# Attention scores accumulated in one PSUM bank from differences of key tiles

## The chip, the cores and the metric

The kernel runs on one core of a Trainium2 chip. The metric is the device time of one execution in microseconds (us). The kernel before took 1691.6 us as the median of three runs (1691.25 to 1692.2).

Engines by the profile's names: PE is TensorE (matmuls; PEld is its loads of stationary weights), DVE is VectorE, ACT is ScalarE, POOL is GpSimd, SP is the engine that issues most DMAs. PSUM has eight banks of 512 float32 columns for each of 128 partitions.

## The reference

```python
xn = layernorm(x)                          # x: 2 x 2048 x 256
q, k, v = split(xn @ w_qkv)                # 16 heads of 16 dimensions
q, k = spectral_filter(q), spectral_filter(k)
attn = softmax(q @ k.T / 4)                # 2048 x 2048 for each of 32 (head, batch)
h = square(relu(xn @ W_fc.T)); y = h @ W_proj.T
spikes = mean of five leaky steps on y
out = x + (attn @ v) @ w_out + b_out + spikes
```

The spectral filter is folded into the query and key weights. All arithmetic is float32 in kind: queries and keys are split in a high and a low part, so that one pass of the faster matmul format on 64 rows (16 dimensions, four products of parts) gives a score.

## The kernel before, in words

A first stage of some 112 us normalises x, projects queries and keys (stored to a scratch in HBM, `qk_scratch`) and values, and finds maxima for the first head. The last stage, some 30 us, multiplies by `w_out` and stores. Between them lie 32 heads (16 heads, 2 batches each; "head" below means one of the 32), and the change is in these.

The softmax subtracts for each query the maximum over all keys. So each head's scores are computed twice. The first time queries lie on the partitions (`maximum`, L711, products of 64x512), and DVE reduces each row (L1017, L1023, L1036) to `pmax`. After half a head's maxima a chain of four short DVE operations (`split_shift`, L1058 to L1073) makes the negated maxima in two parts, and SP spreads them by 8 small DMAs (`store_shift`, L329) to `shift_rows`. These maxima run ahead of the scores by `LEAD`. The second time keys lie on the partitions: `scores` (L718) opens a sum in PSUM and `shifted` (L724) adds to it the product of ones with `shift_rows`. ACT takes the exponential (L562) to `probs`, and `times_v` (L735) multiplies by the values, of which a further column of ones gives the denominator.

One step is 128 keys by 1024 queries. A head has 32 steps. PE's order is written out by hand in `pair` (two steps): 4 products for maxima, 4 for scores, 4 for shifts, 4 product parts of the feed-forward layer (`up` L841, `down` L846), and 8 products with the values, each of 256 columns. All but the last kind use 64 of the 128 rows, and two of them, one in each half of the rows, run side by side. Products with the values use 32 of the columns each, and four run side by side; a float32 product shows as two records.

Six PSUM banks form three slots of two banks (`ring`), which rotate between maxima and scores. ACT copies half of every second slot of maxima to SBUF (`take_half`, L568) for DVE. Two more banks hold the attention output (`po`) and the feed-forward results (`misc`).

SP's queue is in order. In each head (function `head` of the SP block) it issues 8 DMAs of keys (L310), 8 of queries (L320), 16 of shifts (L329) and 8 that move the attention output (L339), with waits on `exp_done`, `shift_turned` and `out_turned` between them. POOL runs the five leaky steps and squares the feed-forward values.

Of the kernel before, what the change touches and what calls it, by code (L numbers as in the profile page):

```python
# [33 lines left out]
STEPS = 2 * TB  # L34
LEAD = 8
FIRST_MAX = 2 * (UNITS - LEAD)
ALONE = STEPS * (B * H - 1) + LEAD
LAG = 2
PRESETS = 7
WARM = 10  # L40
FIRST = 6
PS = 4
# [7 lines left out]
SHIFT = 8 * 16  # L50
SIDE = 4 * DH
SPIKES = 5
AFTER_COPY = (2, 10, 26)
# [16 lines left out]
def build(nc, x, wqk, wv, wout, bout, logits, wfc, wproj, dft, eye, out):  # L70
    with ExitStack() as ctx:
# [3 lines left out]
        def sem(name):  # L75
# [3 lines left out]
        qk_dram = nc.dram_tensor("qk_scratch", [2, H, DH, 2, TOK], F32, kind="Internal").ap()  # L79

# [6 lines left out]
        kst = [sb(f"kst{i}", [P, S], F32R) for i in range(2)]  # L87
        shift_rows = sb("shift_rows", [P, S], F32R)
        ones = sb("ones", [P, P], F32R)
        probs = sb("probs", [P, PS, HALF])  # L90
# [3 lines left out]
        wout_sb = sb("wout_sb", [P, KC, D])  # L94
        bout_sb = sb("bout_sb", [P, D])
# [9 lines left out]
        half_sb = sb("half_sb", [P, BLK])  # L105
# [13 lines left out]
        xt = probs[:, 0:2, :].rearrange("p b (k d) -> p b k d", k=KT)  # L119
        hilo = [[t.rearrange("p (c t) -> p c t", c=2) for t in  # L120
                 (probs[:, 2, :], probs[:, 3, :], relu_sb[:, :, :].rearrange("p f t -> p (f t)"),
# [11 lines left out]
        assert at <= NT * D // 2  # L133

# [15 lines left out]
        def late_copy(g):  # L150

            return FIRST < g < ALONE and g % STEPS in AFTER_COPY

        places = {}
        for g in range(0, STEPS * B * H, 2):
            if g >= ALONE:
                at = [places[ALONE - 2][1], places[ALONE - 2][2], places[ALONE - 2][0]]
                places[g] = (None, at[(g - ALONE) % 3], at[(g + 1 - ALONE) % 3])
            elif g == 0:
                places[g] = (0, 1, 2)  # L160
            else:
                even_max_at, even_score_at, odd_score_at = places[g - 2]
                places[g] = ((even_score_at, even_max_at, odd_score_at) if late_copy(g) else
                             (even_score_at, odd_score_at, even_max_at))

        def copies_until(g):
            return sum(late_copy(k) for k in range(0, g + 1, 2))

        def score_slot(g):
            return ring[:, places[g - g % 2][1 + g % 2], :]  # L170

        def unit_slot(g):
            return ring[:, places[g - g % 2][0], :]
# [114 lines left out]
        def _(sp):  # L288
# [57 lines left out]
            for t in range(NB):  # L346
# [8 lines left out]
                if t == NB - 2:  # L355
                    sp.wait_ge(preset, PRESETS)
                    store_shift(0, 0)
# [901 lines left out]
```

## Time and profile before

| | before |
|---|---|
| median of three runs | 1691.6 us |
| span of the profiled execution | 1689.3 us |
| PE busy (matmuls) | 1681.4 us, x17842 |
| PEld busy (weight loads) | 1145.9 us |
| DVE busy | 1494.2 us, x2375 |
| ACT busy | 1330.1 us, x1718 |
| POOL busy | 719.7 us |
| granted TensorE clock | 1.000 |
| DMA | 108.02 MB, mean 64 GB/s |

The span runs from the first to the last instruction of the profiled execution; its own time is not listed beside it, and the median of the runs is 2.3 us above the span. Busy time is the time in which at least one instruction of the engine was under way. Two matmuls that run side by side count once. In a row of the timeline the first number is the start, the second the length of the whole group (xN instructions), and the brackets give the idle time before it and what ended that.

### The profile page before, as it was taken

How to read it: one execution, taken by the hardware profiler on the slowest of the kernel's cores; microseconds unless marked ns; L12 is line 12 of the kernel's file. 1: busy time of each engine (PE TensorE's matmuls, PEld its weight loads, DVE VectorE, ACT ScalarE, POOL GpSimd, SP SyncE). 2: the span in 40 equal slices, each digit the busy share in tenths (PEclk: the TensorE clock that was granted, in tenths of full speed). 3: DMA queues.
4: the chain of work that ended last, by engine and by line, in shares of the span. 5: the costliest groups of instructions: out<-in, count | busy, mean ns of one | idle time of the engine just before them, and what ended most of it. 6: DMA issues, size and time to landing. Idle time of an engine off the chain costs nothing.

```text
span 1689.3 us, 44435 instructions
## 1 busy us (share of the span) xinstructions
PE 1681.4 (100%) x17842; PEld 1145.9 (68%) x17842; DVE 1494.2 (88%) x2375; ACT 1330.1 (79%) x1718; POOL 719.7 (43%) x979
## 2 busy tenths in 40 slices
PE   9999999999999999999999999999999999999999
PEld 6566666666666666666666666666666666666667
DVE  6889999998999999989998999999989998999884
ACT  5548888888888888888888888888888888888872
POOL 3103334555433345554333455543335554333455
PEclk9999999999999999999999999999999999999999
DMA  6851122112211221122112211221122112211133
GB/s 216 294 161 47 33 54 55 51 33 55 55 50 34 55 55 43 41 55 55 43 41 55 56 37 47 55 55 36 48 55 56 31 53 55 55 30 54 43 105 103
DMA packets 95406, 108.02 MB, mean 64 GB/s; under 512 B 56032, under 2 KB 70240, under 8 KB 95200
## 3 DMA queue, kind: packets, MB, share of 16 engines
q1 hardware_dynamic: 91744, 101.97, 21.2%
q10 hardware_dynamic: 3456, 3.21, 0.6%
q8 instruction: 141, 2.31, 0.6%
q14 instruction: 65, 0.53, 0.1%
HBM read 78.91 MB, written 20.97 MB: 59 GB/s over the span
## 4 chain that ended last, share of the span: by engine, by line
PE 98%; DVE 1%; ACT 0%; issue 0%; ACTq 0%; POOL 0%; POOLq 0%
PE banks L735 31%; PE ring L711 22%; PE ring L718 14%; PE ring L724 14%; PE banks L841 7%; PE banks L846 3%; PE banks L659 2%; PE ring L928 2%; PE ring L672 1%; PE ring L645 1%; PE ring L659 1%; PE ring L686 0%; DVE stats L947 0%; DVE attnT L979 0%; ACT xnT L513 0%
## 5 line engine op out<-in xcount | busy, mean ns | idle before, releaser
L562 ACT ACTIVATE probs<-ring 128x1024 f32<-128x1024 f32 x1024 | 1002.1, 1026 | 6.5 <-PE ring L724 6.2
L711 PE MATMUL ring<-kst,qst 64*128 64x512 f32 x2000 | 674.7, 417 | 0.3 <-ACT probs L562 0.3
L735 PE MATMUL banks<-probs,vst 128*32 128x256 f32 x8192 | 548.2, 385 | 0.1
L1036 DVE TENSOR_REDUCE pmax<-ring 128x2 f32<-128x1024 f32 x407 | 497.7, 1223 | 12.7 <-PE ring L711 0.5
L568 ACT ACTIVATE half_sb<-ring 128x512 f32<-128x512 f32 x500 | 299.2, 598 | 261.4 <-PE ring L711 254.1
L718 PE MATMUL ring<-qst,kst 64*128 64x512 f32 x2048 | 493.0, 425 | 0.1
L711 PEld LDWEIGHTS ring<-kst,qst 64*128 64x128 f32 x2000 | 328.3, 184 | 208.3 <-issue 204.6
L1017 DVE TENSOR_REDUCE pmax<-ring 128x1 f32<-128x512 f32 x500 | 345.4, 691 | 88.7 <-PE ring L711 85.1
L724 PE MATMUL ring<-shift_rows,ones 64*128 64x512 f32 x2048 | 422.9, 390 | 0.0
L1023 DVE TENSOR_REDUCE pmax<-half_sb 128x1 f32<-128x512 f32 x500 | 335.5, 671 | 37.0 <-ACT half_sb L568 33.1
L735 PEld LDWEIGHTS banks<-probs,vst 128*32 128x32 f32 x8192 | 213.7, 109 | 209.7 <-issue 91.0
L841 PE MATMUL banks<-xnT,wfc_sb 64*128 64x128 f32 x2024 | 331.7, 284 | 0.1
L464 POOL TENSOR_TENSOR lif<-lif 128x256 f32<-128x256 f32 x32 | 19.7, 614 | 729.6 <-ACT y_sb L586 729.6
L846 PE MATMUL banks<-wproj_sb,hid_sb 64*128 64x256 f32 x1024 | 329.0, 401 | 0.0
L841 PEld LDWEIGHTS banks<-xnT,wfc_sb 64*128 64x128 f32 x2024 | 280.6, 186 | 19.6 <-PE ring L711 0.4
L718 PEld LDWEIGHTS ring<-qst,kst 64*128 64x128 f32 x2048 | 233.4, 185 | 26.5 <-ACT probs L562 3.6
L724 PEld LDWEIGHTS ring<-shift_rows,ones 64*128 64x128 f32 x2048 | 214.8, 185 | 17.2
L846 PEld LDWEIGHTS banks<-wproj_sb,hid_sb 64*128 64x128 f32 x1024 | 169.6, 184 | 10.9
L474 POOL TENSOR_SCALAR lif<-lif 128x256 f32<-128x256 f32 x128 | 110.1, 860 | 10.8
L475 POOL TENSOR_SCALAR lif<-lif 128x256 f32<-128x256 f32 x128 | 110.6, 864 | 8.0
L473 POOL TENSOR_TENSOR lif<-lif 128x256 f32<-128x256 f32 x128 | 95.1, 743 | 10.0
L471 POOL TENSOR_TENSOR lif<-lif 128x256 f32<-128x256 f32 x128 | 94.3, 737 | 10.0
(96 smaller groups left out, 1050.9 us busy)
## 6 DMA issues: line engine op xcount, KB each, us to landing
kst<-qk_scratch SPq DMA_DIRECT2D x256, 128.0 KB, 3.0
qst<-qk_scratch SPq DMA_DIRECT2D x256, 128.0 KB, 2.9
qk_scratch<-attnT SPq DMA_DIRECT2D x32, 256.0 KB, 3.0
shift_rows<-shiftT SPq DMA_DIRECT2D x512, 2.0 KB
qk_scratch<-probs SPq DMA_DIRECT2D x16, 256.0 KB, 3.0
attnT<-o_turned SPq DMA_DIRECT2D x256, 16.0 KB, 1.9
xnT<-x SPq DMA_DIRECT2D x8, 512.0 KB, 5.6
out<-xnT SPq DMA_DIRECT2D x7, 512.0 KB, 2.9
```

Of the source, the lines that this page charges most:

```text
L475: pool.tensor_scalar(decayed, mem, BETA, None, ALU.mult).then_inc(lif_step, 1)
L562: act.activation(probs[:, s % PS, :], score_slot(g), ACT.Exp, scale=SCALE).then_inc(exp_done, 1)
L568: act.activation(half_sb[:], unit_slot(2 * p)[:, BLK:2 * BLK], ACT.Copy).then_inc(half_taken, 1)
L711: return pe.matmul(unit_slot(g)[:, c * BLK:(c + 1) * BLK], qst[b][rows, tile * P:(tile + 1) * P], kst[b][rows, key:key + BLK], start=True, ...
L718: pe.matmul(score_slot(g)[:, c * BLK:(c + 1) * BLK], kst[b][rows_of(side), kt * P:(kt + 1) * P], qst[b][rows_of(side), q:q + BLK], start=T ...
L724: mm = pe.matmul(score_slot(g)[:, c * BLK:(c + 1) * BLK], ones[rows_of(side), :], shift_rows[rows_of(side), q:q + BLK], start=False, stop= ...
L735: mm = pe.matmul(po[32 * j:32 * (j + 1), half * D:(half + 1) * D], vst[b][:, kt, :], quarters[:, j], start=(kt == 0), stop=(kt == TB - 1))
L841: return pe.matmul(misc[:, (f % 4) * P:(f % 4 + 1) * P], wfc_sb[rows_of(side), c, f * P:(f + 1) * P], xnT[rows_of(side), c, tile * P:(tile ...
L846: return pe.matmul(misc[:, 0:D], hid_sb[rows_of(side), f, :], wproj_sb[rows_of(side), f, :], start=(f == 0 and side == 1), stop=(f == FC - ...
L1017: dve.tensor_reduce(pmax[:, tile, 2 * part:2 * part + 1], unit_slot(g)[:, 0:BLK], AX, ALU.max).then_inc(mx_taken, 1)
L1023: dve.tensor_reduce(pmax[:, tile, 2 * part + 1:2 * part + 2], half_sb[:], AX, ALU.max).then_inc(half_max, 1)
L1036: dve.tensor_reduce(pmax[:, tile, 2 * part:2 * part + 2], unit_slot(g).rearrange("p (c e) -> p c e", c=2), AX, ALU.max).then_inc(mx_taken, 1)
```

## The change

Scores are now computed in places of 512 queries by 128 keys ("mini-steps", 64 in a head), each in one PSUM bank. Three banks (1, 4, 5) serve the scores in turn, three others (0, 2, 3) the maxima. In each quarter of 512 queries the first three key tiles are computed as before, a score product and a shift product (`first_score`). From the fourth on, the bank still holds the score of the key tile three before, shift included, and one product of the queries with the difference of the two key tiles is added to it (`next_score`). The exponential reads the bank between the two.

The differences come from a new path: SP loads the keys in 16 DMAs (`load_stage`), POOL subtracts and adds (`subtract_keys`), ACT rounds to the high part (`high_delta`), POOL makes the low part (`low_delta`), SP stores both in 8 DMAs (`store_delta`) and loads them in three pieces of 4 DMAs each to `delta_sb` (`load_delta`). That is for each head.

PE's order is written anew in groups of four mini-steps ("quads"): `opening_quad` once in each quarter, `later_quad` three times. Products with the values are made for four mini-steps together, of 128 columns each. DVE reduces each maximum's bank by itself (`next_max`), and the copies by ACT are gone. Beside the reductions DVE splits the shifts after mini-steps 15 and 47, takes the outputs from PSUM after 35 and after 3 of the next head, and turns them after 55 and after 23. `w_out` and `b_out` share their buffer with the staged keys and are loaded late.

```diff
-LEAD = 8
+LEAD = 16
-PS = 4
+PS = 8
+CHAINS = 3
+PLACES = 3
+SCORE_BANKS = (1, 4, 5)
+MAX_BANKS = (0, 2, 3)
...
+            def load_stage(u):
...
+                for seg in range(SEGS):
+                    for k in range(2):
+                        at = b * S + k * HOP + seg * SEG
+                        sp.dma_start(stage[seg * DH:(seg + 1) * DH, k, :, :],
+                                     qk_dram[1, h, :, :, at:at + SEG]).then_inc(staged, 16)
+            def store_delta(u):
...
+                for seg in range(SEGS):
+                    sp.dma_start(delta_dram[u % 2, :, :, seg * SEG:(seg + 1) * SEG],
+                                 delta_pair[seg * DH:(seg + 1) * DH]).then_inc(delta_stored, 16)
+            def load_delta(u, piece):
...
+                for group in range(4):
+                    sp.dma_start(delta_sb[group * 2 * DH:(group + 1) * 2 * DH, cols].bitcast(F32),
+                                 src).then_inc(delta_in[piece], 16)
...
             def head(h, b, last=False):
                 i = 2 * h + b
+                sp.wait_ge(exp_done, MINI * i + QUAD)
                 if i and not last:
...
                     load_keys(h + b, 1 - b, 1)
+                if not last:
+                    load_stage(i + 1)
                 store_shift(2 * i + 1, 1)
                 if i:
                     move_output(i - 1, 1)
                 if i and not last:
                     load_queries(h + b, 1 - b, 1)
                 if h < H - 1:
-                    sp.wait_ge(exp_done, STEPS * i + TB + 2)
+                    sp.wait_ge(exp_done, MINI * i + MINI // 2 + QUAD)
                     load_queries(h + 1, b, 0)
...
                 if not last:
+                    store_delta(i + 1)
                     store_shift(2 * i + 2, 0)
+                if h < H - 1:
+                    sp.wait_ge(exp_done, MINI * i + MINI - TB + QUAD)
+                    load_keys(h + 1, b, 0)
                 move_output(i, 0)
-                if h < H - 1:
-                    sp.wait_ge(exp_done, STEPS * i + TB + TB // 2 + 2)
-                    load_keys(h + 1, b, 0)
...
+                if not last:
+                    for piece in range(len(PIECES)):
+                        sp.wait_ge(exp_done, MINI * i + MINI - TB + (piece + 2) * QUAD)
+                        load_delta(i + 1, piece)
...
+            def maximum(x, side):
...
+                pe.wait_ge(mx_taken, n + 3 - PLACES)
+                pe.matmul(max_bank(x), qst[b][rows, tile * P:(tile + 1) * P], kst[b][rows, chunk * BLK:(chunk + 1) * BLK],
+                          start=True, stop=True).then_inc(mx_ready, 1)
+            def bank_free(g):
...
+                if g >= CHAINS:
+                    pe.wait_ge(exp_done, g + 1 - CHAINS)
+            def first_score(g, side):
...
+                bank_free(g)
+                pe.matmul(score_bank(g), kst[b][rows, kt * P:(kt + 1) * P], qst[b][rows, q:q + BLK],
+                          start=True, stop=False)
+                pe.matmul(score_bank(g), ones[rows, :], shift_rows[rows, q:q + BLK],
+                          start=False, stop=True).then_inc(score_ready, 1)
+            def next_score(g, side):
...
+                for piece, (lo, hi) in enumerate(PIECES):
+                    if m * P == lo + HOP:
+                        pe.wait_ge(delta_in[piece], PIECE * (u + 1))
+                bank_free(g)
+                at = (kt - CHAINS) * P
+                pe.matmul(score_bank(g), delta_sb[rows, at:at + P], qst[b][rows, q:q + BLK],
+                          start=False, stop=True, skip_group_check=True).then_inc(score_ready, 1)
+            def times_v(first, last):
+                pe.wait_ge(exp_done, last + 1)
...
+                    for j in range(4):
+                        mm = pe.matmul(po[32 * j:32 * (j + 1), quarter * P:(quarter + 1) * P], vst[u % 2][:, kt, :],
+                                       quarters[:, j], start=(kt == 0), stop=(kt == TB - 1))
...
+            def opening_quad(u, quarter):
+                g, near, far = MINI * u + TB * quarter, 1, 0
+                maximum(g, far)
+                first_score(g, near)
+                first_score(g + 1, far)
+                share(u, quarter, 0, 0)
+                share(u, quarter, 0, 1)
+                maximum(g + 1, far)
+                share(u, quarter, 0, 2)
+                maximum(g + 2, far)
+                share(u, quarter, 0, 3)
+                maximum(g + 3, far)
+                first_score(g + 2, near)
+                next_score(g + 3, far)
+                if g:
+                    times_v(g - QUAD, g - 1)
+            def later_quad(u, quarter, n):
+                g, near = MINI * u + TB * quarter + QUAD * n, 1 - n // 2
+                far = 1 - near
+                maximum(g, far)
+                next_score(g, near)
+                share(u, quarter, n, 0)
+                next_score(g + 1, far)
+                maximum(g + 1, far)
+                share(u, quarter, n, 1)
+                share(u, quarter, n, 2)
+                maximum(g + 2, far)
+                next_score(g + 2, far)
+                share(u, quarter, n, 3)
+                next_score(g + 3, near)
+                maximum(g + 3, far)
+                times_v(g - QUAD, g - 1)
```

## Rows read from the trace of the kernel before

**Rows 1.** Busy us by stretch: PE, PEld, DVE, ACT, POOL, clock, DMA share, GB/s.

```profile
800.00:900.00 100.00, 100.00 (x1130) 68.49 (x1132) 90.39 (x139) 82.72 (x106) 46.36 (x63) 1.00 0.18 47
```

**Rows 2.** Timeline (start, us, engine, line): one pair of steps, PE and DVE.

```profile
800.96 0.18 PEld L711 LDWEIGHTS ring<-kst,qst 64*128 64x128 f32 x1 [0.41 <-issue]
800.96 0.49 PE L711 MATMUL ring<-kst,qst 64*128 64x512 f32 x1
...
801.49 0.69 DVE L1017 TENSOR_REDUCE pmax<-ring 128x1 f32<-128x512 f32 x1 [0.20 <-PE ring L711]
...
803.00 0.59 PEld L735 LDWEIGHTS banks<-probs,vst 128*32 128x32 f32 x16
803.00 1.07 PE L735 MATMUL banks<-probs,vst 128*32 128x256 f32 x16
...
804.00 0.18 PEld L711 LDWEIGHTS ring<-kst,qst 64*128 64x128 f32 x1 [0.41 <-issue]
```

**Rows 3.** Timeline, last head: pairs without maxima, then without feed-forward parts too.

```profile
1642.35 1.07 PE L735 MATMUL banks<-probs,vst 128*32 128x256 f32 x16
...
1644.91 1.07 PE L735 MATMUL banks<-probs,vst 128*32 128x256 f32 x16
...
1652.15 1.07 PE L735 MATMUL banks<-probs,vst 128*32 128x256 f32 x16
...
1654.28 1.07 PE L735 MATMUL banks<-probs,vst 128*32 128x256 f32 x16
```

**Rows 4.** Timeline of PE from 803.0 to 803.3.

```profile
802.68 0.39 PE L711 MATMUL ring<-kst,qst 64*128 64x512 f32 x1
...
803.00 0.64 PE L735 MATMUL banks<-probs,vst 128*32 128x256 f32 x8
```

**Rows 5.** Timeline: a maximum, the split of the shifts, their first DMA.

```profile
807.56 0.69 DVE L1017 TENSOR_REDUCE pmax<-ring 128x1 f32<-128x512 f32 x1 [0.29 <-PE ring L711]
...
808.17 0.18 DVE L1058 TENSOR_REDUCE nmax<-pmax 128x8 f32<-128x32 f32 x1
...
808.92 0.65 DVE L1023 TENSOR_REDUCE pmax<-half_sb 128x1 f32<-128x512 f32 x1
809.03 0.67 SPq L329 DMA_DIRECT2D shift_rows<-shiftT  x1
```

**Rows 6.** Timeline: a weight load that waits for a reduction's bank.

```profile
107.00 1.28 DVE L1012 TENSOR_REDUCE pmax<-ring 128x1 f32<-128x512 f32 x2
107.73 0.19 PEld L645 LDWEIGHTS ring<-kst,qst 128*128 128x128 f32 x1 [0.62 <-DVE pmax L1012]
```

**Rows 7.** Timeline of ACT: 512 columns, then the next.

```profile
1617.78 0.60 ACT L573 ACTIVATE relu_sb<-banks 128x512 f32<-128x512 f32 x1
1618.25 1.04 ACT L562 ACTIVATE probs<-ring 128x1024 f32<-128x1024 f32 x1
```

**Rows 8.** Timeline of SP: shifts and outputs of one half head.

```profile
784.84 5.29 SPq L329 DMA_DIRECT2D shift_rows<-shiftT  x8
790.18 2.58 SPq L339 DMA_DIRECT2D attnT<-o_turned  x4
```

**Rows 9.** Timeline of SP: four DMAs of keys, four of queries.

```profile
165.57 1.82 SPq L310 DMA_DIRECT2D kst<-qk_scratch  x4
...
1592.27 2.51 SPq L320 DMA_DIRECT2D qst<-qk_scratch  x4
```

**Rows 10.** DMA issues: KB each, median us from issue to landing.

```profile
kst<-qk_scratch SPq DMA_DIRECT2D x256, 128.0 KB, 3.0
...
attnT<-o_turned SPq DMA_DIRECT2D x256, 16.0 KB, 1.9
```

**Rows 11.** Timeline of SP and PE where the heads begin.

```profile
99.00 5.36 SPq L329 DMA_DIRECT2D shift_rows<-shiftT  x8
104.40 4.53 SPq L303 DMA_DIRECT2D qk_scratch<-attnT  x8
...
112.80 0.18 PEld L711 LDWEIGHTS ring<-kst,qst 64*128 64x128 f32 x1
```

More of the change, by code:

```diff
@@ L148, in first_part, with chunk_of, bank, score_bank @@
             return TB // 2 + (n - 2 * TB) // 2, n % 2
[L150 to L173, printed above, removed]
-        def unit_of(s):
-            turn, at = divmod((s - LEAD) % UNITS, TB)
-            return turn * TB // 2 + at % (TB // 2), at // (TB // 2)
+        def chunk_of(r):
+            turn, at = divmod(r // 2, TB)
+            return turn * TB // 2 + at % (TB // 2), 2 * (at // (TB // 2)) + r % 2
+        def bank(k):
+            return ring[:, k // 2, k % 2 * BLK:(k % 2 + 1) * BLK]
+        def score_bank(g):
+            return bank(SCORE_BANKS[g % CHAINS])
+        def max_bank(x):
+            return bank(MAX_BANKS[x % PLACES])
         mx = max_slot.rearrange("p (c e) -> p c e", c=2)
@@ L476, in head @@
                     n += 4
+                    if step == 2 and not last:
+                        square(i + 1, 0, UP_A)
                 pool.wait_ge(lif_step, n + 1)
@@ L705, in rows_of @@
                 return slice(side * SIDE, (side + 1) * SIDE)
-            def maximum(g, s, b, c, side):
-                (tile, part), rows = unit_of(s), rows_of(side)
-                key = (2 * part + c) * BLK
-                return pe.matmul(unit_slot(g)[:, c * BLK:(c + 1) * BLK], qst[b][rows, tile * P:(tile + 1) * P],
-                                 kst[b][rows, key:key + BLK], start=True, stop=True)
-            def scores(g, s, b, side, c):
-                half, kt = s // TB, s % TB
-                q = half * HALF + c * BLK
-                pe.matmul(score_slot(g)[:, c * BLK:(c + 1) * BLK], kst[b][rows_of(side), kt * P:(kt + 1) * P],
-                          qst[b][rows_of(side), q:q + BLK], start=True, stop=False)
@@ new lines, in times_v @@
+            def times_v(first, last):
+                pe.wait_ge(exp_done, last + 1)
+                for g in range(first, last + 1):
+                    u, m = divmod(g, MINI)
+                    quarter, kt = divmod(m, TB)
+                    if m % (MINI // 2) == 0:
+                        pe.wait_ge(po_taken, 2 * u + m // (MINI // 2))
+                    if m == 0:
+                        pe.wait_ge(vst_ready, u + 1)
+                    quarters = probs[:, g % PS, :].rearrange("p (t j q) -> p j t q", j=4, q=32)
+                    for j in range(4):
+                        mm = pe.matmul(po[32 * j:32 * (j + 1), quarter * P:(quarter + 1) * P], vst[u % 2][:, kt, :],
+                                       quarters[:, j], start=(kt == 0), stop=(kt == TB - 1))
+                    mm.then_inc(pv_done, 1)
@@ L1140, in _, with beside_maxima @@
             halve(1, pmax[:, TB // 2:TB, 0:2], FIRST_MAX)
[L1141 to L1151 removed]
+            def beside_maxima(i, m, last):
+                h, b = divmod(i, B)
+                if m == 3 and i:
+                    take_output((i - 1) // B, (i - 1) % B, 1)
+                if m == 7 and i:
+                    weigh_output(2 * i - 1)
+                if m == 11 and i:
```

473 lines of the change are left out of this document (189 added, 284 removed).

## The prediction

> **What bounds the kernel now.** I read the busy shares by stretch first, then the timeline of one pair of steps, then the last head's pairs, where parts of the work are missing, and at last SP's queue.
>
> Between 200 and 1600 us every stretch of 100 us looks like [rows 1]: PE busy 100.00 of 100 us, DVE 90.39, ACT 82.72, the granted clock 1.00, which is the 2.4 GHz level. So PE sets the pace, but DVE has only a tenth to give. A pair of steps begins with the weight load at 800.96 and the next at 804.00, so 3.04 us [rows 2], and a head has 16 pairs: 48.6 us. The pair has two parts. From 800.96 to 803.00 run the products on half the rows, two at a time: 12 products of 512 columns and 4 feed-forward parts, so 8 units in each half. From 803.00 to 804.00 run the 16 records with the values. In the last head pairs without their 4 maxima follow at 1642.35 and 1644.91, 2.56 us apart, and pairs without the feed-forward parts too at 1652.15 and 1654.28, 2.13 us apart [rows 3]. So two units less in each half give back 0.48 and then 0.43 us: 0.22 to 0.24 us per unit. PE's time follows the count of units, and this is the scale for the change.
>
> **PE's work after.** A later quad has 4 maxima, 4 scores and 4 feed-forward parts, which the code deals out as 6 units on each half of the rows (near: two scores and the four parts; far: four maxima and two scores). That is the content of the pairs at 2.56 us [rows 3], with maxima in the place of shifts. An opening quad has three shifts more: 8 units on the near half, 7 on the far, so 3.04 us as a pair now.
>
> The values' products change from 16 records of 256 columns to 32 of 128. Two bounds: each record half as long, so nothing changes (0); or each record at the mean pace of the row, 1.00/16 = 0.0625 us, so 1.00 us more per quad. The row inside the group decides: from 803.00 on eight records are begun and done within 0.64 us; if each takes about the 0.39 of the product in the row above it, their starts lie within 0.25 us, 0.036 apart; and 16 weight loads take 0.59 us [rows 2, 4]. So records start faster than 0.0625 where the columns let them, and the pace is that of the columns; I take +0.02 us. The Trainium skill, TensorE: Matmul & The Clock Gate, section "Wait — 56ns, not 53.3ns?", says that with hardware decoding off the sequencer spends about 62 ns on each matmul; 32 records would then need some 2 us in place of 1. The row of eight speaks against it here.
>
> PE alone would need 12 x 2.58 + 4 x 3.06 = 43.2 us for a head, 5.4 less than now.
>
> **The wait for a maximum's bank.** Three banks serve four maxima of a quad, so the fourth needs the reduction of the first. A quad's first load is at 0; DVE starts 0.53 us later (800.96 to 801.49) [rows 2]; a reduction of 512 columns lasts 0.69 us [rows 5]; a load that waits for the end of a reduction starts 0.04 us after it (107.00 + 0.69 to 107.73) [rows 6]. So the fourth maximum's load comes at 1.26 us. Its columns start 0.10 later (a first product takes 0.49 us where a following one takes 0.39), and from the columns of the last such product to the values' load are 0.32 us (802.68 to 803.00) [rows 2, 4]: 1.68 us, and with 1.02 for the values a later quad takes 2.70 us in place of 2.58. If PE's queue loads the weights before the wait it is 2.6; if DVE is late by half a reduction, 3.0. I take 2.70, the value of the rows. In an opening quad the fourth maximum comes late enough anyway.
>
> **DVE.** Reductions of 512 columns follow each other by 0.61 us (807.56 to 808.17) [rows 5], four in 2.44 of 2.70 us. All 64 are now of this size, without help from ACT's copies. The split of the shifts holds DVE for 0.75 us (808.17 to 808.92) [rows 5], twice in a head; 0.26 is idle anyway and 0.1 more hides in the opening quad behind it, so 0.4 us each. The transposes and short operations behind other fourth maxima fit the idle 0.26 us almost; 0 to 0.6, I take 0.2 per head. Sum: 12 x 2.70 + 4 x 3.06 + 0.8 + 0.2 = 45.6 us for a head, 3.0 less than now. DVE would be busy for some 42 of these.
>
> **ACT.** An exponential of 512 columns is not in the trace, but a Relu of that size is: 0.60 us, and the next operation starts after 0.47 [rows 7]. Bounds for four of them are 1.9 and 2.4 us, under 2.70 both; the copies go. A score that needs the bank of three mini-steps before comes at 0.53 + 0.60 + 0.04 = 1.17 us after the quad's start at the earliest, ahead of the fourth maximum's 1.26. Cost 0 while the bank of the maxima is later; POOL's two subtractions of 416 and 208 columns and ACT's copy are done early in the head, cost 0.
>
> **SP's queue.** Now in a head: 16 shifts at 5.29/8 = 0.66, 8 outputs at 2.58/4 = 0.65 [rows 8], 8 key loads at 1.82/4 = 0.46 and 8 query loads at 2.51/4 = 0.63 [rows 9]: 24.4 us. The change adds 12 loads of the differences (form of the key loads, 0.46: 5.5 us), 16 loads and 8 stores of 16 partitions, which the trace does not show: between 0.46 and 0.66, so 11.0 to 15.8 us; I take 0.6, since their patterns have three dimensions as the queries' have. SP is then occupied for 44 of 47 us.
>
> What counts is a chain in this queue. The shifts of the next head's first half are split after maximum 47; behind them SP issues 8 shifts, 4 keys, 4 outputs and then the first piece of the differences, and `next_score` of mini-step 3 of the next head waits for it. Measured from the start of quad 44: the split starts at 0.53 + 4 x 0.61 = 2.97; SP follows 0.86 later (808.17 to 809.03) [rows 5], at 3.8; 8 shifts to 9.1; 4 keys to 11.0; 4 outputs to 13.6; the fourth load of the piece is issued at 15.0. It lands 3.0 us later if as the key loads, 1.9 if as the small output moves [rows 10]; its piece has 80 KB against 128, so nearer the keys: 18.0. PE wants it after quad 44 (2.7), the opening quad 48 (3.06 + 0.4), three quads (8.1), 0.1 for DVE and 1.4 into quad 64: 15.8. PE stands for 2.2 us (1.1 with the short landing). Behind the waiting product stand the values' products and the next quad's maxima, so DVE, kept at the pace of PE, starves as well and nothing is made up. That is in 31 heads. Head: 47.8 us.
>
> The first half of the head holds: SP is free about 1.2 us after PE's wait ends; 4 keys, 16 staged loads of 0.6, 8 shifts and the landing need 18 us, and PE asks for these shifts after 21.1. The point at which this queue would decide is 0.72 us per staged load.
>
> **Beginning and end.** The shifts are issued from 99.00 to 104.36, then come 8 stores of differences (4.8 us), the stores of the last block (4.53), and four loads that land 3.0 after the last: about 118.2, where PE wants them at 112.80 + 0.5 + 1.4 = 114.7 [rows 11]. So +3.5 us, +0.5 for the feed-forward product moved ahead. The last head has 4 pairs of 3.04, 9 of 2.56 and 3 of 2.13 now, 41.6 us; after, 3.06 + 3 x 2.70 with maxima, two quarters of 3.06 + 3 x 2.58, and four quads of about 2.6, where each last score waits for the first exponential (1.17 + 0.4 + 1.02): 43.2, and 2 for the last group of values, of which now 1 is there: +2.6.
>
> Sum: 31 x (47.8 - 48.6) + 3.5 + 0.5 + 2.6 = -18; the span goes from 1689.3 to about 1671, and the median stands 2.3 above the span, so 1673. PE's idle stays at 2 us at a time, at which I expect the granted clock to stay.
>
> **The rivals.** (1) No wait for the differences: the piece lands sooner, or the quads run slower than worked out while the chain does not. Then a head is 45.6: 31 x 2.2 = 68 less, 1605. For it speaks the short landing of small moves; against it that the chain's issue times alone are 11.1 us. If PE's loads also pass the wait for banks, 12 x 0.1 x 31 = 37 less, 1568. (2) SP becomes the bound, slower than before: its place is the 16 staged loads between keys and shifts in the first half. Each 0.1 us above 0.72 puts 1.6 us on a head; at 0.85 that is 2.1 x 31 = 65, so 1738. For it speaks that the load is the queue's largest new part; against it that none of the four forms has a mean above 0.66. (3) DVE and PE lock worse than in my sums, later quads of 3.0 us: nine of the twelve count fully, three lie in SP's chain and shorten its wait, so 9 x 0.3 x 31 = 84 more, 1757. Two engines within 7% of each other speak for it. (4) Records with the values start one by one, 0.0625 us each: 0.98 us on 16 quads, 15.7 less the 2.2 that SP's chain then hides, x 31 = 418: 2091.
>
> **Chances.** The forecast 0.47, rival 1 0.18, rival 2 0.18, rival 3 0.15, rival 4 0.02. The forecast's own range is 1645 to 1705, with the landing and 0.05 us of a later quad either way. A measurement of this kernel can tell about 0.2%, 3.4 us, from no change. Of the forecast's 0.47 I put 0.37 faster, 0.05 the same and 0.05 slower; with the rivals faster 0.56, same 0.06, slower 0.38. The range for 8 in 10 is 1602 to 1745.
>
> **What would show it.** Right: later quads 2.70 us apart by the first record with the values; loads for maxima that wait on DVE for some 0.1 us; in each head's first quad PE idle for about 2 us, released by a DMA to `delta_sb`; ACT under DVE. Wrong: a group with the values of 2 us (rival 4); PE waiting for `shift_rows` at mini-step 32 or SP's staged loads above 0.7 us (rival 2); quads of 3 us without a DMA (rival 3); no DMA among PE's releasers (rival 1). A granted clock under 1.00 would upset every sum.

## The result, and the profile after

| kernel | median of its runs, us | profiled span, us | granted clock |
|---|---|---|---|
| before | 1691.9 (4 runs) | 1689.3 | 1.00 |
| after | 1758.6 (1755.4 to 1762.8, 4 runs) | 1753.6 | 0.977 |

The ratio is 1.040, 95% interval 1.038 to 1.041: slower by 4.0%, where 1673 us was forecast and the range ended at 1745. Against a forecast of 18 us less, the span is 64.3 us longer. Of two kernels below ("staging behind the shifts" and "the two late places") one of four runs lay far from the rest, at 2113 and 5843 us, and is left out.

Busy times of the page, after:

```profile
PE 1634.4 (93%) x24366; PEld 1220.9 (70%) x24366; DVE 1506.6 (86%) x2782; ACT 1177.1 (67%) x2274; POOL 787.4 (45%) x1075
```

The same view as [rows 1], by stretch: PE, PEld, DVE, ACT, POOL, clock, DMA share, GB/s. PE was busy 100.00 of 100 us before and is 92.82 now; in the stretch of 10 us behind 870 the clock is 0.83, so a part of it ran at the 1.2 GHz level.

```profile
800.00:900.00 100.00, 92.82 (x1495) 70.07 (x1495) 87.92 (x160) 69.88 (x136) 47.80 (x64) 0.98 0.29 77
820.00:830.00 10.00, 8.58 (x146) 6.65 (x144) 7.67 (x15) 6.52 (x14) 8.34 (x12) 1.00 0.46 113
870.00:880.00 10.00, 7.00 (x88) 5.34 (x79) 4.99 (x9) 4.27 (x9) 8.33 (x11) 0.83 0.48 127
```

The steady quads are what was forecast. Timeline of PE, after: three groups with the values, 2.71 and 2.72 us apart, and 1.01 us from one group to the product behind it (825.52 to 826.53). At the top stands the product that waited for the differences.

```profile
825.10 0.49 PE L806 MATMUL ring<-qst,delta_sb 64*128 64x512 f32 x1 [1.42 <-DMA delta_sb<-delta_scratch]
825.52 1.08 PE L821 MATMUL banks<-probs,vst 128*32 128x128 f32 x32
826.53 0.49 PE L773 MATMUL ring<-kst,qst 64*128 64x512 f32 x1
...
828.24 1.08 PE L821 MATMUL banks<-probs,vst 128*32 128x128 f32 x32
...
830.95 1.08 PE L821 MATMUL banks<-probs,vst 128*32 128x128 f32 x32
```

In a later quad (weight loads of the quad that starts at 850.52) the fourth score is released by ScalarE 1.22 us after the start and the fourth maximum comes at 1.28, 0.05 behind the end of the first reduction (851.06 + 0.69); the forecast had 1.17 and 1.26.

```profile
851.74 0.18 PEld L806 LDWEIGHTS ring<-qst,delta_sb 64*128 64x128 f32 x1 [0.22 <-ACT probs L626]
851.80 0.18 PEld L773 LDWEIGHTS ring<-kst,qst 64*128 64x128 f32 x1
```

The waits over the whole span (total us, times, longest). The first line is the forecast wait, 69.8/31 = 2.25 us: once in each of heads 1 to 30, and for 1.32 us in head 0. Of the 69 waits of the second line 62 stand in the openings of mini-steps 16 and 48 (means 1.39 and 0.56 us), behind the splits of the shifts. The third is late shift rows, seven times; two of them, 5.79 us in head 0 and 4.54 in head 30, are 10.3 of its 12.0 us.

```profile
PEld ring L806 <- DMA delta_sb<-delta_scratch: 69.8, 31, 3.4
PEld ring L773 <- DVE pmax L1032: 62.1, 69, 1.4
...
PEld ring L792 <- DMA shift_rows<-shiftT: 12.0, 7, 5.8
```

The opening quad of mini-step 16, after: VectorE's split of the shifts has a CAST (L1055) of 1.00 us, beside a square of GpSimd (L507) of 1.04 us, and TensorE's load of weights waits 1.43 us for a reduction behind it. Before, the same CAST had a minimum of 0.17 and a maximum of 0.30 us.

```profile
835.01 0.19 DVE L1051 TENSOR_REDUCE nmax<-pmax 128x8 f32<-128x32 f32 x1
835.23 1.00 DVE L1055 CAST shift<-nmax 128x8 fp32r<-128x8 f32 x1
836.26 0.17 DVE L1058 TENSOR_TENSOR shift<-nmax,shift 128x8 fp32r<-128x8 f32 x1
```

```profile
835.16 1.04 POOL L507 TENSOR_TENSOR hid_sb<-relu_sb 128x512 f32<-128x512 f32 x1 [1.85 <-ACT relu_sb L631]
```

In another head the square starts earlier against the split. The CAST is shorter, and ends again just behind the square (1136.58 and 1136.55).

```profile
1135.51 1.04 POOL L507 TENSOR_TENSOR hid_sb<-relu_sb 128x512 f32<-128x512 f32 x1 [1.44 <-ACT relu_sb L631]
1135.70 0.19 DVE L1051 TENSOR_REDUCE nmax<-pmax 128x8 f32<-128x32 f32 x1
1135.92 0.66 DVE L1055 CAST shift<-nmax 128x8 fp32r<-128x8 f32 x1
```

The load of weights behind the first of the two splits:

```profile
837.30 0.18 PEld L773 LDWEIGHTS ring<-kst,qst 64*128 64x128 f32 x1 [1.43 <-DVE pmax L1032]
```

SP's queue over one head, after (start, us; x is the number of DMAs). The sixteen stagings (L335) are 0.70 us each and the eight stores of differences (L342) 0.75; the shifts are as in [rows 8], the outputs' moves 3.05 and 3.44 against 2.58 there. Of the 50.4 us from the start of the first line to the start of the last SP is occupied for some 49.

```profile
871.93 5.64 SPq L351 DMA_DIRECT2D delta_sb<-delta_scratch  x12
877.61 1.82 SPq L317 DMA_DIRECT2D kst<-qk_scratch  x4
879.47 11.26 SPq L335 DMA_DIRECT2D tail<-qk_scratch  x16
890.77 5.26 SPq L361 DMA_DIRECT2D shift_rows<-shiftT  x8
896.08 3.05 SPq L371 DMA_DIRECT2D attnT<-o_turned  x4
899.17 5.50 SPq L327 DMA_DIRECT2D qst<-qk_scratch  x8
904.71 6.05 SPq L342 DMA_DIRECT2D delta_scratch<-tail  x8
911.56 5.31 SPq L361 DMA_DIRECT2D shift_rows<-shiftT  x8
916.91 1.86 SPq L317 DMA_DIRECT2D kst<-qk_scratch  x4
918.82 3.44 SPq L371 DMA_DIRECT2D attnT<-o_turned  x4
922.38 5.62 SPq L351 DMA_DIRECT2D delta_sb<-delta_scratch  x12
```

Mean lengths of the quads of a head over the trace, from the starts of the groups with the values. The first two rows are means over heads 1 to 31, the other quads over heads 0 to 30, and the last row over heads 1 to 30, so the column does not add up exactly:

| part of a head | forecast, us | after, us |
|---|---|---|
| opening 0, with the wait for the differences | 5.26 | 5.33 |
| the quad behind it | 2.70 | 3.46 |
| opening 16 | 3.46 | 4.26 |
| opening 32 | 3.06 | 3.53 (median 3.00; head 0 10.69, head 30 8.98) |
| opening 48 | 3.46 | 3.67 |
| eleven later quads | 29.7 | 30.1 (median of one quad 2.72) |
| transposes | 0.2 | inside the rows above |
| head | 47.8 | 50.1 |

### The profile page after: what moved, and what is told of

Its sections match the earlier page's. It is cut to its first block, busy times and chain, and to the rows that moved or that the text cites. A ratio compares the mean times of both kernels' runs of the same rounds, so it can differ in the third digit from the quotient of the medians.

```text
span 1753.6 us, 60281 instructions
## 1 busy us (share of the span) xinstructions
PE 1634.4 (93%) x24366; PEld 1220.9 (70%) x24366; DVE 1506.6 (86%) x2782; ACT 1177.1 (67%) x2274; POOL 787.4 (45%) x1075
## 4 chain that ended last, share of the span: by engine, by line
PE 62%; DVE 16%; SPq 13%; DMA 4%; issue 3%; ACT 2%; ACTq 0%; POOL 0%; DVEq 0%; POOLq 0%
PE banks L821 22%; PE ring L773 14%; DVE pmax L1032 11%; PE ring L806 10%; PE banks L831 6%; SPq L361 4%; DMA delta_sb<-delta_scratch 4%; PE banks L826 3%; SPq L351 3%; DVE shift L1055 2%; SPq L371 2%; SPq L335 2%; ACT probs L626 2%; PE ring L942 2%; SPq L317 1%
## 5 line engine op out<-in xcount | busy, mean ns | idle before, releaser
L626 ACT ACTIVATE probs<-ring 128x512 f32<-128x512 f32 x2048 | 1076.0, 601 | 485.2 <-PE ring L806 303.7
L1032 DVE TENSOR_REDUCE pmax<-ring 128x1 f32<-128x512 f32 x2000 | 1246.5, 681 | 106.6 <-PE ring L773 98.1
L773 PE MATMUL ring<-kst,qst 64*128 64x512 f32 x2000 | 812.6, 451 | 42.3 <-DVE pmax L1032 42.3
L806 PE MATMUL ring<-qst,delta_sb 64*128 64x512 f32 x1664 | 607.9, 454 | 58.0 <-DMA delta_sb<-delta_scratch 56.4
L821 PE MATMUL banks<-probs,vst 128*32 128x128 f32 x16384 | 564.8, 279 | 0.0
L821 PEld LDWEIGHTS banks<-probs,vst 128*32 128x32 f32 x16384 | 424.1, 111 | 141.9 <-ACT probs L626 99.2
L806 PEld LDWEIGHTS ring<-qst,delta_sb 64*128 64x128 f32 x1664 | 283.1, 189 | 122.1 <-DMA delta_sb<-delta_scratch 69.8
L792 PE MATMUL ring<-qst,kst 64*128 64x512 f32 x384 | 156.0, 470 | 10.0 <-DMA shift_rows<-shiftT 10.0
L522 POOL TENSOR_TENSOR lif<-lif 128x256 f32<-128x256 f32 x32 | 19.6, 612 | 247.3 <-ACT y_sb L646 247.3
L507 POOL TENSOR_TENSOR hid_sb<-relu_sb 128x512 f32<-128x512 f32 x64 | 66.5, 1039 | 141.7 <-ACT relu_sb L631 141.7
L794 PE MATMUL ring<-shift_rows,ones 64*128 64x512 f32 x384 | 128.0, 394 | 0.0
L529 POOL TENSOR_TENSOR lif<-lif 128x256 f32<-128x256 f32 x128 | 94.1, 735 | 10.0
```

Source lines behind the costliest of these rows:

```text
L529: pool.tensor_tensor(mem, upd, spks[(step + 1) % 2], ALU.subtract).then_inc(lif_step, 1)
L626: act.activation(probs[:, g % PS, :], score_bank(g), ACT.Exp, scale=SCALE).then_inc(exp_done, 1)
L773: pe.matmul(max_bank(x), qst[b][rows, tile * P:(tile + 1) * P], kst[b][rows, chunk * BLK:(chunk + 1) * BLK], start=True, stop=True).then_i ...
L792: pe.matmul(score_bank(g), kst[b][rows, kt * P:(kt + 1) * P], qst[b][rows, q:q + BLK], start=True, stop=False)
L794: pe.matmul(score_bank(g), ones[rows, :], shift_rows[rows, q:q + BLK], start=False, stop=True).then_inc(score_ready, 1)
L806: pe.matmul(score_bank(g), delta_sb[rows, at:at + P], qst[b][rows, q:q + BLK], start=False, stop=True, skip_group_check=True).then_inc(sco ...
```

## The experiments

Three places looked costly: the differences' load behind the output's move, the square beside the split, and the 24 small DMAs on SP. Each was changed alone, then in all pairs, then all three.

**Order.** In the head's part of SP:

```diff
+                if not last:
+                    sp.wait_ge(exp_done, MINI * i + MINI - TB + 2 * QUAD)
+                    load_delta(i + 1, 0)
                 move_output(i, 0)
                 if not last:
-                    for piece in range(len(PIECES)):
+                    for piece in range(1, len(PIECES)):
```

> The first piece of the differences is loaded ahead of the move of an output on SP's queue, instead of behind it; nothing else changes. The output's four issues took 3.0 us of SP between the end of a head's last reads of the old differences and the load. Theory A (the loss is three stalls on TensorE: the wait for the differences of 2.25 us in each head, the fall of the granted clock that follows it at about 1.0 us a head, and the split of mini 16 held by the square on GpSimd at 0.84 us): the first two go, about 3.2 us in each of 31 heads, so some 100 us less than the changed kernel's 1758.6: 1660 us, and the granted clock is 1.00 in the heads. Theory B (SP's queue, with about 49 us of work in a head of 50, is the bound, and the stalls only show it): the wait goes from the differences but comes back somewhere else, at the shift rows of mini 32 or 0, and a head stays at 49 us or more: 1725 us or more.

Measured 1768.6 us (1761.2 to 1774.4), 10 slower than the changed kernel. The forecast wait is gone (opening 0 has 3.03 us, the quad behind it 2.71, medians), and another has come, at the shift rows of mini-step 32: its opening went from 3.00 to 5.90 us (medians), and the halved clock with it.

```profile
PEld ring L795 <- DMA shift_rows<-shiftT: 79.3, 31, 7.8
...
PEld ring L809 <- DMA delta_sb<-delta_scratch: 15.9, 28, 1.3
```

Theory A (stalls that add up) falls here; theory B named the place, and the time lies 44 us above its "1725 or more". Why it is 10 us worse than without the edit, and not equal, is open.

**Square.** In GpSimd's part:

```diff
+                pool.wait_ge(shift_turned, 2 * i + 2)
                 square(i, 1, UP_B)
```

> GpSimd starts its second square of a head only after VectorE's split of the shifts at mini 16, with which it ran at the same time before; nothing else changes. Theory A: the CAST of that split falls from 1.00 us to the 0.17 of the other splits, the opening of mini 16 from 4.30 us to about 3.46, 0.84 us in each head, 26 us in all: 1732 us. Theory B (SP's queue is the bound): the opening becomes shorter, but the wait for the differences later in the head grows by as much: 1750 to 1759 us. Third possibility: the CAST stays long with no square beside it, so something else held it.

Measured 1750.4 us (1748.9 to 1753.6): 8 less. The CAST's mean over both splits fell from 654 to 260 ns (0.17 us at mini-step 16; the other split's is 0.35 in both kernels) and the opening of 16 from 4.30 to 3.47, just what was expected of it. But the mean of opening 0 grew from 5.33 to 5.60 and of opening 32 from 3.53 to 3.95, which takes up most of it: B.

```profile
L1055 DVE CAST shift<-nmax 128x8 fp32r<-128x8 f32 x64 | 41.8, 654 | 2.2
```

```profile
L1056 DVE CAST shift<-nmax 128x8 fp32r<-128x8 f32 x64 | 16.6, 260 | 2.2
```

(The changed kernel, then this one.)

**Fewer.** The same bytes staged by 4 DMAs of 128 partitions, stored by 2:

```diff
-                for seg in range(SEGS):
-                    for k in range(2):
-                        at = b * S + k * HOP + seg * SEG
-                        sp.dma_start(stage[seg * DH:(seg + 1) * DH, k, :, :],
-                                     qk_dram[1, h, :, :, at:at + SEG]).then_inc(staged, 16)
+                for k in range(2):
+                    at = b * S + k * HOP
+                    for r in range(2):
+                        sp.dma_start(stage[:, k, r, :],
+                                     qk_dram[1, h, :, r, at:at + DELTA].rearrange("d (s x) -> s d x", x=SEG)).then_inc(staged, 16)
```

> The keys for the differences are staged by 4 DMAs instead of 16, and the differences stored by 2 instead of 8, with the same bytes; SP's queue in a head falls from about 49 us by some 12 (18 issues fewer at 0.70 us). The output's move still stands ahead of the differences' load. Theory A: the wait for the differences of 2.25 us in each head stays, and with it the fall of the clock and the opening of mini 16; only the late shift rows of the first head (7.7 us) and of the head before the last go: 1745 to 1755 us. Theory B: SP's queue was the bound, and a head falls from 50.1 to the 47 to 48 of TensorE's own work: 1680 to 1700 us.

Measured 1772.1 us (1760.7 to 1774.5): 13 slower with less to do. The staged keys now come while the square runs, so GpSimd's subtraction follows it directly and VectorE's next operation (L1058) is held as well; the opening of 16 takes 5.11 us (median), and from 130 us on the clock is halved for 113 us instead of 79. Timelines of VectorE and GpSimd in this kernel:

```profile
843.90 0.99 DVE L1055 CAST shift<-nmax 128x8 fp32r<-128x8 f32 x1
844.93 0.98 DVE L1058 TENSOR_TENSOR shift<-nmax,shift 128x8 fp32r<-128x8 f32 x1
```

```profile
843.83 1.04 POOL L507 TENSOR_TENSOR hid_sb<-relu_sb 128x512 f32<-128x512 f32 x1 [3.63 <-ACT relu_sb L631]
844.83 1.06 POOL L483 TENSOR_TENSOR tail<-tail 128x416 f32<-128x416 f32 x1
```

Neither theory had this. A was right that the wait for the differences stays when the queue is short (65.0 us, 30 times), and that the late shift rows go: the opening of 32 is 3.00 in heads 0 and 30 too.

**Warm.** Ahead of the wait for the differences:

```diff
+                if m == CHAINS and u:
+                    bank_free(g)
+                    for _ in range(5):
+                        pe.matmul(score_bank(g)[:, 0:D], lif[:, 4, 0:P], lif[:, 4, :], start=False, stop=False,
+                                  skip_group_check=True)
```

> While TensorE waits for the differences of the next head it first runs five products with zeros, added to the bank of scores that it writes next (the result is the same). The wait ends when it did. Theory A with the clock as a cause of its own: TensorE is busy for longer just before the quads that ran at half clock, the clock stays at 1.00, and the quad behind the first of a head goes from a median of 3.67 us to 2.72: about 1.0 us in each of 31 heads, 30 us in all: 1728 us. If the clock does not depend on this pause the time stays at 1758, or goes up by the products, 1 us a head at most. Theory B (SP's queue is the bound): the clock comes back, but the time gained is waited for the differences again: 1750 to 1760 us.

Measured 1750.8 us (1749.6 to 1752.4). The granted clock over the span is 0.994 instead of 0.977, and the quad behind the opening is 2.72 in the median. But the five products run as ten records that last 2.43 us, longer than the wait, and set the opening to 5.81 in most heads (5.35 before): mean 0.74 us back on the one quad, 0.66 lost on the other. The time fits theory B's 1750 to 1760, but not by its reason, a longer wait for the differences. The clock's part was right, the price of the probe too low.

```profile
820.32 2.43 PE L804 MATMUL ring<-lif 128*128 128x256 f32 x10
823.17 0.50 PE L811 MATMUL ring<-qst,delta_sb 64*128 64x512 f32 x1 [0.42 <-DMA delta_sb<-delta_scratch]
```

**Order and fewer.**

> The two edits together that made it slower one by one: the first piece of the differences loaded ahead of the output's move (alone: 1768.6 us), and staging and storing of the differences by 6 DMAs instead of 24 (alone: 1772.1). Theory C (both stand in a ring: the place of the load behind the output costs 2.25 us a head, and with this gone SP's 49 us of work a head hold the shift rows of mini 32 by 2.7 us; either alone leaves the other): now neither wait is left, quads of 2.72 and openings of 3.03, 5.11 (mini 16, with the subtraction on GpSimd now beside the split), 3.00 and 3.66: 12 x 2.72 + 14.8 = 47.4 us a head against 50.1, about 85 us in all: 1675 us. If each edit does harm for a reason of its own, the harms add up: 1780 us.

Measured 1648.4 us (1645.1 to 1652.6), 0.974 of before (0.972 to 0.976). Two edits that cost 10 and 13 us alone bring 110 together: theory C, though 27 us better than its sum, for the most part as the opening of 16 was 4.30 again in most heads and not 5.11.

**All three.**

> All three edits: differences loaded ahead of the output, 6 DMAs instead of 24, and GpSimd's second square (with the subtraction behind it) only after VectorE's split of mini 16. Theory C: the opening of mini 16 falls from 5.1 to the 3.47 that it had with this edit alone, and nothing takes it up, since SP's queue has room: 12 x 2.72 + 3.03 + 3.47 + 3.00 + 3.66 = 45.8 us a head, 1.6 less than with two edits: about 1625 us, the granted clock 1.00 in the heads, and the kernel ahead of the one before the change (1691). If GpSimd's delay makes its own chain (subtraction, square, store of the differences) late, the gain is less: 1650 us or more.

Measured 1625.4 us (1623.0 to 1627.0), ratio to before 0.960 (0.959 to 0.962). The openings are 3.03, 3.47, 3.00 and 3.66, most heads 45.8. SP now has room in each head, and PE's busy share is 98%.

```profile
PE 1588.1 (98%) x24366; PEld 1192.4 (74%) x24366; DVE 1476.7 (91%) x2782; ACT 1171.8 (72%) x2274; POOL 788.8 (49%) x1075
```

**Square and fewer, then with the products of zeros.** These price the place of the load alone, and the clock alone, with room on SP.

> Two of the three edits: 6 DMAs instead of 24 for the differences, and GpSimd's square behind VectorE's split of mini 16; the load of the differences stands behind the output's move as in the changed kernel. SP's queue has room here, so what remains over the kernel with all three edits (1625.4 us) is the price of that place alone, with the fall of the clock that follows. Theory C: first quad 5.35 us and the quad behind it 3.7 instead of 3.03 and 2.72, so 3.3 us a head more, 31 times: about 1728 us. If the place cost only its own 2.3 us, 1697 us.

> The same two edits, and five products with zeros ahead of the wait for the differences (the result is the same). SP's queue has room, so what the clock gives back can't be taken by another wait, as it was when the products stood in the changed kernel. If the fall of the clock comes from TensorE's pause and costs 1.0 us a head, this is 30 us faster than the same kernel without the products (1728 expected, so 1698), with the granted clock 1.00 in the heads. If the products themselves end later than the wait did, up to 0.5 us a head of this is lost (15 us).

Measured 1695.1 us (1688.0 to 1703.3, 10 runs) and 1700.3 (1699.4 to 1701.4). So the place of the load, with the clock behind it, costs 69.7 us over all three edits.

```profile
PEld ring L807 <- DMA delta_sb<-delta_scratch: 64.5, 30, 3.2
```

The first time is near the 1697 that stood for no price of the clock, but that is partly luck. In the traces the opening is 2.1 us longer than with all three edits (5.19 against 3.07, 66 us in all) and the quad behind it 0.5 (3.23 against 2.72, 16 us), and the kernel with all three edits gives some back in its next quad (3.02 against 2.84). The clock's price was expected too high: half clock for 48 us in this trace, and the quad behind the opening falls from a mean of 3.23 to 2.71 with the zeros, 0.5 us a head. The zeros held the opening at 5.81 and cost more than that, so the expected 30 us less did not come.

**Order and square.**

> The other two edits: differences loaded ahead of the output, and GpSimd's square behind the split; staging and storing by 24 DMAs as in the changed kernel. SP has 49.4 us of issues a head. If its queue is the bound when it is that long, a head is 49.4 us or more although TensorE's own work is 45.8: about 1740 us, with the wait at the shift rows of mini 32, 3 us or more. If its length doesn't matter once the order is right, the time is near 1625 us.

Measured 1773.2 us (1769.8 to 1777.9): with the fewer DMAs alone the slowest of the eight combinations; the opening of 32 takes 6.96 (median).

```profile
PEld ring L796 <- DMA shift_rows<-shiftT: 101.4, 31, 8.0
```

SP's queue over a head (from 802.82 to 853.60, 50.8 us) has 48.8 us of issues and one wait of 1.4 us, for the split of mini-step 48:

```profile
802.82 5.26 SPq L361 DMA_DIRECT2D shift_rows<-shiftT  x8
808.13 2.57 SPq L371 DMA_DIRECT2D attnT<-o_turned  x4
810.74 5.79 SPq L327 DMA_DIRECT2D qst<-qk_scratch  x8
816.57 5.34 SPq L342 DMA_DIRECT2D delta_scratch<-tail  x8
823.29 5.31 SPq L361 DMA_DIRECT2D shift_rows<-shiftT  x8
...
843.04 10.51 SPq L335 DMA_DIRECT2D tail<-qk_scratch  x16
853.60 5.25 SPq L361 DMA_DIRECT2D shift_rows<-shiftT  x8
```

**Staging behind the shifts, twice.** Is it the sum of the issues, or their order? From the last kernel:

```diff
-                if not last:
-                    load_stage(i + 1)
                 store_shift(2 * i + 1, 1)
+                if not last:
+                    load_stage(i + 1)
```

> The kernel with differences ahead of the output and the square behind the split (24 DMAs, 1773.2 us), with one more move: in each head the 16 DMAs that stage the keys are issued behind the shift rows of the second half instead of ahead of them. SP's queue is as long as before. Theory R (a ring through two engines: from the split of mini 48 SP issues shifts, keys, differences, output, keys, staging and shifts of mini 32, 35.6 us; TensorE waits there for these shifts and comes to the next split 15.2 us later; 50.8 us a head): the staging's 10.5 us leave the ring, which then takes 40.3 us, less than TensorE's 45.8, so the wait at mini 32 goes, and what is left as a bound is the sum of SP's issues, 48.9 us a head: 2 us a head less, 1711 us. If the sum of the issues were the bound already, nothing changes: 1770 us. If neither bounds, 1625 us.

Measured 1883.4 us (1880.8 to 1884.2, three runs), outside all three forecasts. The wait at the shift rows went, but the keys now come later, and ScalarE, which has its part of the differences at mini-step 35, waits for them with the exponentials behind it:

```profile
854.98 0.38 ACT L597 ACTIVATE tail<-tail 128x208 fp32r<-128x208 f32 x1 [6.50 <-POOL tail L488]
```

The repeat moves this part from `2 * TB + 3` to `2 * TB + 14`:

> The kernel with the staging behind the shift rows (1883.8 us), with ScalarE's part of the differences behind the exponential of mini 46 instead of mini 35, where it waited 6.5 us in each head for the staged keys and held the exponentials behind it. Eleven mini steps are 7.5 us, so ScalarE finds the keys there. Then neither the ring (40.3 us) nor this wait is left, and by theory R the sum of SP's issues is the bound, 48.9 us a head: 1711 us. If the place of a SP wait does not matter and the old time of 1773 comes back, theory R is wrong about the ring. If SP's sum does not bound either, 1625 us.

Measured 1857.9 us (1855.2 to 1862.4), heads of 53.5. All three forecasts missed. SP comes to the shifts of 32 before they are split and stands for 4.4 us (815.02 + 1.81 to 821.24); the staging used to fill this time. What stands behind in the queue is late by it, and TensorE now waits for the queries and for the differences.

```profile
815.02 1.81 SPq L317 DMA_DIRECT2D kst<-qk_scratch  x4
821.24 5.27 SPq L361 DMA_DIRECT2D shift_rows<-shiftT  x8
826.55 11.21 SPq L335 DMA_DIRECT2D tail<-qk_scratch  x16
```

```profile
PEld ring L777 <- DMA qst<-qk_scratch: 91.7, 30, 4.9
PEld ring L810 <- DMA delta_sb<-delta_scratch: 84.1, 39, 3.9
```

Here a head of 53.5 us has 48.6 us of issues and 4.4 of standing; in the kernel before the move one of 50.8 has 48.8 and 1.4 (the rest are gaps of about 0.05 between the groups). That issues and standing add up to a head is so in any order; what the runs add is that the standing changes with the order. So both count. With 24 small DMAs no head can be shorter than SP's issues, some 49 us, and the heads measured are 49.9 to 54.4. What they have above that is time in which SP waits, for a split above all (150.9 us in the last run), while TensorE waits for what stands behind it in the queue. The proposed ring, as it was priced, named neither 1884 nor 1858 us; how the amount comes about is not shown, and no run put these DMAs on another engine's queue.

**Without differences.** First scores everywhere (`first_score` in place of `next_score`), and no staging, storing or loading of differences; SP also waits one quad longer before it loads the next head's keys.

> The quads, banks and queues of the change, but every score is computed anew with its own key tile (two products with the shift, as for the first three tiles): no product with differences, and no staging, storing or loading of differences. The result is the same. It shows what the differences alone are worth. SP has some 23 us less work a head, TensorE one product more in 13 of 16 key tiles: quads of 3.06 us (the pitch before) instead of 2.72. Expected: 12 x 3.06 + 3.1 + 4.6 + 3.1 + 3.9 = 51.4 us a head, no wait at the head's end, clock 1.00: about 1780 us. If it is below 1758, the differences cost more than they saved; if it comes to 1691, the change's other parts cost nothing.

Measured 1771.5 us (1770.7 to 1772.8), clock 1.00, heads of 50.77. The new quads and openings alone cost 79 us over the kernel before: quads of 3.09 against 3.04 for a pair, and openings of 3.44, 3.18 and 3.90. The differences give 146 us over this when nothing waits for them, and 13 as they were put in.

**The two late places.** Shifts ahead of the staging in every head, and the loads of x for the end behind the shifts of head 30, on top of the three edits.

> The three edits, and the two places that were late once: the shift rows of the second half are stored ahead of the staging in every head, and the six loads of x for the end stand behind the shifts of the head before the last. Against the three edits: the opening of mini 32 in head 0 (10.7 us in the changed kernel) and in head 30 (9.0) goes to 3.0 as far as it is still late. With the shorter staging most of this is gone already, so 0 to 8 us under the kernel with three edits: about 1618 us.

Measured 1623.7 us (1621.9 to 1626.1, three runs), no difference from the three edits. In those the opening of 32 was already 3.00 in head 0 and 4.05 in head 30; here it is 3.00 in both.

The eight combinations, medians in us:

| | as in the change | fewer DMAs |
|---|---|---|
| as in the change | 1758.6 | 1772.1 |
| order | 1768.6 | 1648.4 |
| square | 1750.4 | 1695.1 |
| order and square | 1773.2 | 1625.4 |

## Why the prediction was wrong

**Later quads, 2.70: right** (2.71 to 2.72 in most). The wait for the maximum's bank was built from starts of three rows and held to 0.02 us. **The values' records, +0.02: right**; the groups take 1.01 us. So rivals 3 and 4 are out, and ACT stayed under VectorE, though by 0.06 us only (1.22 and 1.28).

**Wait for the differences, 2.2 a head: right** in the changed kernel (2.25), and again with SP's queue short (64.5 / 30 = 2.15, square and fewer).

**Split, 0.4 each: wrong at mini-step 16.** It cost 1.2: the sum took VectorE's split as alone, and in the new timing a square of GpSimd falls on it. That is 0.80 us a head in the trace, and moving the square took 22.9 us off the two-edit kernel (0.74 a head). At mini-step 48 the opening has 0.21 us too much; the CAST takes 0.35 there in place of the 0.17 of the other split, and the sum used one split for both. The Trainium skill, SBUF — State Buffer, section "Who interferes with whom", says that VectorE and GpSimd share a port pair that one of them holds for a whole instruction, and counts casts and operations with two SBUF inputs among those that can be held, reductions not. The traces agree: the CAST of 8 columns lasts 1.00 us beside the square, or as long as the square is still under way (0.66 at 1135.92), a TENSOR_TENSOR 0.98 beside the subtraction, while the reduction at 1135.70 takes its 0.19 inside the square, and all 31 reductions of 512 columns that fall inside it take 0.69.

**Clock at 1.00: wrong.** The sum said that PE stands for 2 us at a time and that the clock would stay. It fell to the 1.2 GHz level behind 19 of the 31 waits, for 3.4 us mostly: 0.76 a head on the quad behind (3.46 against 2.70). With products in the pause that quad was back at 2.72.

**SP's queue, 44 of 47 us: wrong in a size, and so rival 2 was priced on its own and not with the rest.** The stagings took 0.70 instead of 0.6 and the stores 0.75, outputs up to 3.4 in place of 2.6: about 49 us. The limit of 0.72 for a staging was loose too: keys, 16 stagings of 0.6 and shifts are 16.7 of the 18 us, which leaves 1.3 for the landing, and with the 1.9 of the small moves in [rows 10] the limit is 0.68. In the changed kernel this hardly shows as a wait for shift rows, since TensorE's other stalls make the head 50.1; the queue is the floor under them. It shows when a stall is removed: order or square alone brings nothing or harm, and order and square together 1773. The forecast's best case (rival 1, heads of 45.6, 1605 us) needed this floor gone; with the three edits the heads are 45.8 and the time 1625.

**Beginning and end.** Up to the first group with the values in head 1 the span grew by 13.5 us against 3.2 in the sum: the 16 stagings stand ahead of head 0's shift rows, and the opening that waits for them took 10.69 us (3.00 with the fewer DMAs). The end grew by 1.7, forecast 2.6. With the heads between (30 heads, +49.0 against -24) this is the 64.3 us.

In short, by the 82 us between forecast and span: about 23 from the clock behind the wait, 24 from the square on the split, 6 from the opening of 48, 14 from the late shift rows of heads 0 and 30, 13 from the eleven later quads (30.1 against 29.7; in 10 of 30 heads the first of them takes 2.9 to 3.3, for a reason that no run isolated), the rest small terms and rounding. These are means over the trace; the runs confirm the first by its return in the quads alone, as the products that kept the clock cost about as much, and the second by time, but only where SP has room.

## What to carry to other kernels

Where a queue of DMA issues is nearly as long as the work it serves, count it before any stall: a removed stall comes back at the next thing that queue delivers, so try the fix together with a shorter queue. When timing moves, check which operations of VectorE and GpSimd newly fall on each other. An issue that is moved later drags the engines that wait for it in their own order, so follow it to the last reader.

## What the runs showed of the hardware

A DMA issue occupied SP's queue for a mean of 0.45 to 0.86 us in the groups shown, by its form but not by its bytes: key loads of 128 KB took 0.46, stagings of 26 KB 0.70. So 4 issues of 128 partitions in place of 16 of 16 partitions were 2.6 us against 11.3, with the same bytes. The price is not quite fixed: with the fewer DMAs the 8 query loads took 7.8 us in place of 5.5.

The length of TensorE's pause alone did not decide over the clock. Behind the 31 waits for the differences (load of weights, 1.32 to 3.42 us) it fell to half 19 times: behind one of 1.88 us (before 1375.91) it did, behind one of 2.43 (before 477.60) it stayed.
